# The row-column step of the expert stage: half of its products replaced by TensorE transposes

## The chip, the cores and the metric

The kernel runs on one core of a Trainium2 chip. The metric is the time of one launch on the device in microseconds. Engines are named as in the profile: PE (TensorE matmul), PEld (TensorE weight load), DVE (VectorE), ACT (ScalarE), POOL (GpSimd), SP (SyncE, here only the issuer of DMAs).

## What is computed

The input `x` holds 32 images of 64 channels and 56 by 56 positions, in float32. First comes a convolution block per image: a layer norm over the channels, a 3x3 convolution and a 1x1 convolution of signs with binarized weights, batch norms and leaky activations. Its result is added to `x`. Then each of the 100,352 positions is a token of 64 numbers that goes through a routed feed-forward layer with eight experts:

```python
logits = x @ gate_w + gate_b
probs = softmax(logits, axis=-1)
idx = argmax(probs, axis=-1)
...
hmid = relu(einsum('ecd,edf->ecf', buf, w1) + b1)   # 64 -> 256
ybuf = einsum('ecf,efd->ecd', hmid, w2) + b2         # 256 -> 64
y_tok = ybuf[idx, pos_g] * (prb * kept)
```

The result, scaled by the gate and with its infinities and NaNs replaced, is added to the tokens and stored in the layout of the images.

## The kernel before, in words

Two images form a pair: one lies on partitions 0 to 63, the other on 64 to 127. The first half of the program (up to some 970 us) does the convolution block for 16 pairs in a software pipeline, transposes the result to rows of tokens, routes them, and scatters *row pairs* to DRAM: a row pair is a token of the first image and the token of the second image at the same position. Row pairs are sorted by the two experts that they need, into groups (36 of them), each padded to blocks of 256 row pairs (SUPER = 256, in SUB = 2 parts of P = 128).

The second half is the **expert stage**: 231 blocks ("supers", NSUP), one after the other. Every engine runs its own `super_pass`, a software pipeline over the supers; the order of the work on an engine is written out by hand, and semaphores tie the engines together. In the pass k, PE (lines 810 to 845) does four steps:

- t, line 817, for super k+1: the **row-column step**. The rows of the super lie in SBUF as `RTH` (128 row pairs on the partitions; for each of the two images h, C = 64 numbers and three more). Four products with the identity matrix turn them into columns: for each part d and each image h, the 128x64 rows are the weights, the 128x128 identity is streamed, and the 64x128 result goes to the PSUM bank `PT`, image 0 on partitions 0 to 63 and image 1 on 64 to 127. The last product increments `s_pt`.
- l1, line 826, for super k: four products of the first expert layer, two for each image, with 64 rows of weights each (`HC` = 4). It waits until ACT has copied the columns of super k to `XT` (`s_xt`), and until ACT and DVE have emptied the hidden banks of super k-1 (`s_ha`, `s_hb`).
- l2, line 836, for super k-1: four products of the second layer, to 64 PSUM partitions each.
- back, line 844, for super k-2: two 128x128 transposes of the results, to rows.

A float32 product is carried out as two records of LDWEIGHTS and MATMUL, a float32 transpose as one: line 817 has 1848 records of each (231 x 4 x 2), line 844 has 462 (231 x 2).

Around them: SP loads the rows and the weights of a super twelve supers ahead (lines 600 to 610). ACT copies PT to XT (line 973), does three of the four ReLUs (line 980), adds the output bias (line 990) and widens the results (line 985). DVE does the fourth ReLU (line 1294) and the gating (lines 1307 to 1316). POOL scatters the results (line 524), held back by `s_pt` to a place six supers behind PE's row-column step. From super 62 on, seven of every twelve supers are followed on PE by an image group (`image_group`, line 855: four transposes of finished tokens back to image layout), whose sums DVE does (line 1323).

Of the kernel before, what the change touches and what calls it, by code (L numbers as in the profile page):

```python
# [14 lines left out]
def metaformer_kernel(nc, x, move1, w3, g1, be1, mu1, va1, pm1, ps1, pb1, move2, w_pw,  # L15
# [6 lines left out]
    IMAGES, C, H, W = x.shape  # L22
# [3 lines left out]
    P = 2 * C  # L26
# [83 lines left out]
    with ctx:  # L110
        def sb(name, shape, dt=fp32):
            return ctx.enter_context(nc.sbuf_tensor(name, shape, dt))
# [60 lines left out]
        ident = sb("ident", [P, P])  # L173
# [32 lines left out]
        RTH = RT.rearrange("p r j (h w) -> p r j h w", h=2)  # L206
# [119 lines left out]
        def wait(eng, s, count):  # L326

            if isinstance(count, int) and count <= 0:
                return
            eng.wait_ge(s, count)  # L330

        def wait_apart(eng, s, count):


            wait(eng, s, count)
            if not isinstance(count, int):
                eng.sem_inc(s_past, 1)
# [45 lines left out]
        def hidden(q):  # L383

            return (bank[2][:, 0:SUPER], bank[3][:, 0:SUPER], bank[2][:, SUPER:2 * SUPER], bank[4][:, 0:SUPER])[q]
# [283 lines left out]
        def _(pe):  # L669
            mm = nc.tensor.matmul  # L670
# [137 lines left out]
            PT, YT, YB = bank[0], bank[5], bank[7]  # L808

            def super_pass(k, ring, lap, t=True, l1=True, l2=True, back=True):  # L810
                if t:
                    u = (ring + 1) % RING
                    wait(pe, s_rt[u], (lap + (ring + 1) // RING) * 32 + 32)
                    wait_apart(pe, s_xt, k + 1)
                    for d in range(SUB):
                        for h in range(2):
                            last = mm(PT[h * C:h * C + C, d * P:(d + 1) * P], RTH[:, u, d, h, 0:C], ident[:, :],  # L817
                                      start=True, stop=True)
                    last.then_inc(s_pt, 1)
                if l1:  # L820
                    wait(pe, s_xt, k + 1)
                    wait(pe, s_ha, k)
                    wait(pe, s_hb, k)
                    for q in range(HC):
                        b = slice(q % 2 * C, q % 2 * C + C)
                        mm(hidden(q), WR[b, ring, q // 2 * P:(q // 2 + 1) * P], XT[b, ring % 2, :],  # L826
                           start=True, stop=True).then_inc(s_h, 1)
                if l2:
                    b = (ring - 1) % RING
                    wait(pe, s_ha, k)  # L830
                    wait(pe, s_hb, k)
                    wait(pe, s_ys, k - 1)
                    for q in range(HC):
                        h = q % 2
                        at = W2_AT + (h * KT + q // 2) * C
                        last = mm(YT[h * C:h * C + C, 0:SUPER], WR[:, b, at:at + C], HB[:, b % 2, q, :],  # L836
                                  start=q < 2, stop=q >= HC - 2)
                    last.then_inc(s_y, 1)
                if back:
                    b = ring % 2  # L840
                    wait(pe, s_ys, k - 1)
                    wait_apart(pe, s_g, (k - 3) * GSTEPS + 1)
                    for d in range(SUB):
                        last = nc.tensor.transpose(YB[:, d * P:(d + 1) * P], YS[:, b, d * P:(d + 1) * P], ident[:, :])  # L844
                    last.then_inc(s_yb, 1)
            super_pass(-1, -1 % RING, -1, l1=False, l2=False, back=False)
            super_pass(0, 0, 0, l2=False, back=False)
            super_pass(1, 1, 0, back=False)
            def image_group(q, odd, g):
                if g == 0:  # L850
# [517 lines left out]
```

## Time and profile before

| | |
|---|---|
| median of 3 runs (lowest to highest) | 1802.32 us (1801.11 to 1811.1) |
| profiled execution | 1805.56 us |
| its span, first to last instruction | 1803.6 us |
| PE busy | 1558.0 us (86%) |
| DVE busy | 1467.3 us (81%) |
| ACT busy | 1236.8 us (69%) |
| POOL busy | 1052.6 us (58%) |
| granted TensorE clock, mean | 0.921 |

The busy time of an engine is the part of the span in which one of its instructions is under way. Matmul records overlap, since the next one is streamed while the last one drains, and their ends are modelled; so on PE starts say more than ends. A timeline merges neighbouring records of one line and shape into one row with their count, the start of the first, and the time that they cover together. The granted clock is 1.00 at 2.4 GHz and 0.50 at 1.2 GHz.

### The profile page before, as it was taken

The numbers are of one execution on the slowest core, as the hardware profiler recorded it, in microseconds if no ns is written. First come the engines' busy times: TensorE is split into PE (matmuls) and PEld (weight loads), VectorE is DVE, ScalarE is ACT, GpSimd is POOL, SyncE is SP. The second block draws the span as 40 slices with busy tenths as digits, with TensorE's granted clock in tenths as the row PEclk, the third lists the DMA queues.
The fourth block names the chain that finished last, engine by engine and source line by source line (L and its number), as shares of the span: only waits on it lengthen the run. The fifth ranks groups of instructions, "written<-read, shape, count | busy, mean of one in ns | idle before, by whom it ended". The sixth has DMA issues, their size and how long they took to land.

```text
span 1803.6 us, 39937 instructions
## 1 busy us (share of the span) xinstructions
PE 1558.0 (86%) x10341; PEld 838.7 (47%) x10341; DVE 1467.3 (81%) x3641; ACT 1236.8 (69%) x4066; POOL 1052.6 (58%) x1052
## 2 busy tenths in 40 slices
PE   6998989888888898887740599999999999999994
PEld 1344434334343344443330355556666666666662
DVE  3588888888888888978882388889999999999995
ACT  4788786777777878777640377777676666776661
POOL 3115666666577666676667266666556565666662
PEclk8999988989998999987765799999999999999996
DMA  9446868676476773554422777788999999999995
GB/s 239 84 106 131 179 153 173 150 165 158 116 163 153 131 152 122 119 121 108 118 77 79 233 199 195 199 235 243 299 281 299 296 321 296 302 309 288 298 303 206
DMA packets 302219, 351.75 MB, mean 195 GB/s; under 512 B 48453, under 2 KB 252453, under 8 KB 295941
## 3 DMA queue, kind: packets, MB, share of 16 engines
q1 hardware_dynamic: 260644, 264.23, 55.6%
q0 software_dynamic: 41120, 85.81, 15.8%
q14 instruction: 101, 0.82, 0.1%
q8 instruction: 34, 0.56, 0.1%
q10 hardware_dynamic: 320, 0.33, 0.1%
HBM read 179.70 MB, written 180.01 MB: 199 GB/s over the span
## 4 chain that ended last, share of the span: by engine, by line
PE 49%; DVE 19%; issue 13%; POOL 8%; ACT 5%; DMA 4%; SPq 1%; POOLq 0%; ACTq 0%; DVEq 0%
PE bank L826 11%; PE bank L836 10%; PE bank L817 6%; POOL pairs_by_group L492 5%; PE bank L735 5%; PE bank L844 4%; PE bank L697 3%; PE bank L794 3%; DVE ROWS L1323 3%; DMA pairs_by_group<-ROWS,idx 2%; POOL X L486 2%; PE bank L745 2%; PE bank L768 2%; ACT SQR L960 1%; DVE X L1294 1%
## 5 line engine op out<-in xcount | busy, mean ns | idle before, releaser
L492 POOL DMA_INDIRECT pairs_by_group<-ROWS,idx x400 | 436.3, 1091 | 119.5 <-issue 113.2
L524 POOL DMA_INDIRECT results_by_pair<-X,PAIRNO x310 | 307.8, 993 | 220.6 <-PE bank L817 128.6
L980 ACT ACTIVATE X<-bank,X 128x256 f32<-128x256 f32 x693 | 283.7, 472 | 59.9 <-PE bank L826 59.9
L486 POOL TENSOR_TENSOR X<-Z,X 128x448 f32 (+1 forms) x112 | 140.2, 1252 | 268.6 <-DVE Z L1271 251.8
L826 PE MATMUL bank<-X 64*128 64x256 f32 x1848 | 263.4, 403 | 9.6 <-DVE X L1294 5.6
L836 PE MATMUL bank<-X 128*64 128x256 f32 x1848 | 250.4, 392 | 1.0 <-DVE X L1294 1.0
L735 PE MATMUL bank<-S,WB 128*128 128x448 bf16 x1008 | 231.6, 378 | 0.0
L973 ACT ACTIVATE X<-bank 128x256 f32<-128x256 f32 x231 | 88.8, 384 | 197.6 <-PE bank L817 196.7
L524 POOL DMA_INDIRECT results_by_pair<-S,PAIRNO x152 | 153.3, 1008 | 97.0 <-PE bank L817 70.2
L817 PE MATMUL bank<-ident,X 128*64 128x128 f32 x1848 | 153.3, 287 | 58.6 <-DMA X<-weights_by_group 58.1
L826 PEld LDWEIGHTS bank<-X 64*128 64x128 f32 x1848 | 163.1, 187 | 59.8 <-issue 46.3
L960 ACT ACTIVATE SQR<-bank 128x64 f32<-128x64 f32 (+1 forms) x800 | 168.8, 259 | 0.0
L960 ACT ACTIVATION_READ_ACCUMULATOR SQR<-bank 128x1 f32 (+1 forms) x800 | 167.1, 245 | 0.0
L735 PEld LDWEIGHTS bank<-S,WB 128*128 128x128 bf16 x1008 | 95.6, 102 | 152.6 <-issue 72.6
L836 PEld LDWEIGHTS bank<-X 128*64 128x64 f32 x1848 | 112.1, 136 | 110.8 <-issue 77.5
L1294 DVE TENSOR_SCALAR X<-bank,X 128x256 f32<-128x256 f32 x231 | 110.4, 478 | 60.7 <-PE bank L826 60.2
L697 PE MATMUL bank<-X,row_weights 128*128 (+1 forms) x224 | 126.7, 653 | 32.4 <-ACT SQ L908 23.6
L817 PEld LDWEIGHTS bank<-ident,X 128*64 128x64 f32 x1848 | 97.2, 137 | 95.3 <-DMA X<-weights_by_group 59.1
L764 PE MATMUL bank<-biasrow,ones 65*128 65x432 bf16 x144 | 51.6, 358 | 98.7 <-POOL X L486 50.3
L768 PE MATMUL bank<-row_weights,X 128*128 128x144 f32 x800 | 134.7, 308 | 0.0
L917 ACT ACTIVATE N<-Z,cst 128x448 f32 (+1 forms) x112 | 76.7, 685 | 84.1 <-DVE Z L1231 83.6
L768 PEld LDWEIGHTS bank<-row_weights,X 128*128 128x128 f32 x800 | 128.9, 209 | 5.1 <-issue 0.2
(213 smaller groups left out, 3045.9 us busy)
## 6 DMA issues: line engine op xcount, KB each, us to landing
X<-weights_by_group SPq DMA_DIRECT2D x231, 258.5 KB
X<-pairs_by_group SPq DMA_DIRECT2D x231, 134.0 KB
pairs_by_group<-PAD SPq DMA_DIRECT2D x15, 1742.0 KB
X<-in_x_dram SPq DMA_DIRECT2D x16, 1568.0 KB, 8.0
block_output<-X SPq DMA_DIRECT2D x112, 224.0 KB, 4.5
ROWS<-block_output SPq DMA_DIRECT2D x16, 1568.0 KB
Z<-results_by_pair SPq DMA_DIRECT2D x16, 1568.0 KB, 9.9
out_dram<-ROWS SPq DMA_DIRECT2D x16, 1568.0 KB
```

The source lines that it names most:

```text
L486: pool.tensor_tensor(X2[:, j * CW:(j + 1) * CW], Z[:, p.z(j * CW)], X[:, p.x(j * CW, CW)], ALU.add).then_inc(s_x2, 1)
L492: pool.indirect_dma_start(rows, bass.IndirectOffsetOnAxis(ap=idx[0:m, p.odd, k:k + 1], axis=0), ROWS[0:m, p.odd, k, :], None).then_inc(s_s ...
L524: pool.indirect_dma_start(done, bass.IndirectOffsetOnAxis(ap=PAIRNO[:, u, j:j + 1], axis=0), RES[u][:, j, :], None,).then_inc(s_back[u], 16)
L697: mm(centered(c, alone)[:, 0:CW], center[:, :], X[:, cen.x(c * CW, CW)], start=True, stop=True).then_inc(s_cen, 1)
L735: last = mm(CONV[(con.odd + c) % 2][:, 0:CW], WB[:, t, :], S1[:, con.odd, c * CHUNK_ROWS + dy:(c + 1) * CHUNK_ROWS + dy, dx:dx + W], start ...
L768: last = mm(ROWP[g][:, at:at + GW], X2[:, k * P:(k + 1) * P], row_weights[:, :], start=False, stop=k == group_tiles[g][-1])
L817: last = mm(PT[h * C:h * C + C, d * P:(d + 1) * P], RTH[:, u, d, h, 0:C], ident[:, :], start=True, stop=True)
L826: mm(hidden(q), WR[b, ring, q // 2 * P:(q // 2 + 1) * P], XT[b, ring % 2, :], start=True, stop=True).then_inc(s_h, 1)
L836: last = mm(YT[h * C:h * C + C, 0:SUPER], WR[:, b, at:at + C], HB[:, b % 2, q, :], start=q < 2, stop=q >= HC - 2)
L960: last = A(SQR[0:m, (odd * NG + g) % 2, i, h * C:h * C + C], src[0:m, i, h * C:h * C + C], ACT.Square, accum_out=SSQ[0:m, odd, k:k + 1])
L980: last = A(HB[:, ring % 2, q, :], hidden(q), ACT.Relu, bias=WR[:, ring, at:at + 1])
L1294: V.tensor_scalar(HB[:, ring % 2, q, :], hidden(q), WR[:, ring, at:at + 1], 0.0, ALU.add, ALU.max).then_inc(s_hb, 1)
```

## The change

In the row-column step, the two products of image 0 (h = 0) become two calls of TensorE's transpose, with the same operands and the same place in PSUM; the two products of image 1 stay. The order stays too: d = 0 with both images, then d = 1 with both images; the increment of `s_pt` stays on the last product.

```diff
                     wait_apart(pe, s_xt, k + 1)
                     for d in range(SUB):
                         for h in range(2):
-                            last = mm(PT[h * C:h * C + C, d * P:(d + 1) * P], RTH[:, u, d, h, 0:C], ident[:, :],
-                                      start=True, stop=True)
+                            if h == 0:
+                                nc.tensor.transpose(PT[0:C, d * P:(d + 1) * P], RTH[:, u, d, 0, 0:C], ident[:, :])
+                            else:
+                                last = mm(PT[C:P, d * P:(d + 1) * P], RTH[:, u, d, 1, 0:C], ident[:, :],
+                                          start=True, stop=True)
                     last.then_inc(s_pt, 1)
```

## Rows read from the trace of the kernel before

**Rows 1.** The page: span, busy time of PE, 40 slices of PE and its clock.
```profile
span 1803.6 us, 39937 instructions
...
PE 1558.0 (86%) x10341; PEld 838.7 (47%) x10341; DVE 1467.3 (81%) x3641; ACT 1236.8 (69%) x4066; POOL 1052.6 (58%) x1052
...
PE   6998989888888898887740599999999999999994
...
PEclk8999988989998999987765799999999999999996
```
**Rows 2.** Windows: from:to, length, busy of each engine (records), clock, DMA share, GB/s.
```profile
0.00:870.00 870.00, 755.62 (x3600) 342.41 (x3600) 703.42 (x1500) 654.56 (x2467) 502.43 (x506) 0.92 0.64 143
...
1011.00:1204.00 193.00, 192.16 (x1632) 113.90 (x1632) 153.71 (x483) 145.84 (x373) 113.83 (x117) 0.98 0.76 217
1204.00:1757.00 553.00, 544.03 (x4705) 340.28 (x4704) 506.47 (x1424) 384.16 (x998) 334.24 (x334) 1.00 0.93 294
```
**Rows 3.** Waits of PE, 1011 to 1757 us: total, times, longest.
```profile
PE bank L817 <- DMA X<-weights_by_group: 58.1, 1, 58.1
PE bank L826 <- DVE X L1294: 5.0, 12, 0.7
PE bank L826 <- ACT X L973: 2.8, 5, 0.6
```
**Rows 4.** Timeline of PE, a super without an image group: start, time covered, line.
```profile
1407.08 0.44 PE L844 MATMUL bank<-ident,X 128*128 128x128 f32 x2
1407.45 0.66 PE L817 MATMUL bank<-ident,X 128*64 128x128 f32 x8
1408.04 1.14 PE L826 MATMUL bank<-X 64*128 64x256 f32 x8
1409.10 1.08 PE L836 MATMUL bank<-X 128*64 128x256 f32 x8
1410.12 0.44 PE L844 MATMUL bank<-ident,X 128*128 128x128 f32 x2
```
**Rows 5.** Timeline of PE, a super with an image group.
```profile
1399.99 0.44 PE L844 MATMUL bank<-ident,X 128*128 128x128 f32 x2
1400.27 0.55 PE L855 MATMUL bank<-ident,Z 112*128 112x112 f32 x4
1400.75 0.66 PE L817 MATMUL bank<-ident,X 128*64 128x128 f32 x8
```
**Rows 6.** Timeline of PE at 703 us: float32 products on the whole array.
```profile
702.99 0.90 PE L768 MATMUL bank<-row_weights,X 128*128 128x144 f32 x6
```
**Rows 7.** Groups of instructions of PE, 702.75 to 704.9 us: busy, mean ns.
```profile
L768 PE MATMUL bank<-row_weights,X 128*128 128x144 f32 x12 | 1.8, 285 | 0.0
```
**Rows 8.** Groups of instructions of PE, 1204 to 1757 us.
```profile
L817 PE MATMUL bank<-ident,X 128*64 128x128 f32 x1328 | 109.2, 285 | 0.0
L844 PE MATMUL bank<-ident,X 128*128 128x128 f32 x334 | 73.0, 300 | 0.0
L855 PE MATMUL bank<-ident,Z 112*128 112x112 f32 x385 | 52.9, 259 | 0.0
```
**Rows 9.** Timeline of PE in the setup: products, then transposes, all 128 wide.
```profile
21.47 0.28 PE L681 MATMUL bank<-gw,row_weights 128*128 128x8 f32 x2
21.61 1.29 PE L686 MATMUL bank<-ident,X 128*128 128x128 f32 x10
```
**Rows 10.** Timeline of DVE: the same instruction in two supers with image groups.
```profile
1397.27 0.50 DVE L1294 TENSOR_SCALAR X<-bank,X 128x256 f32<-128x256 f32 x1
...
1400.81 0.50 DVE L1294 TENSOR_SCALAR X<-bank,X 128x256 f32<-128x256 f32 x1
```
**Rows 11.** Waits of ACT, 1011 to 1757 us.
```profile
ACT X L973 <- PE bank L817: 195.9, 225, 62.1
```
**Rows 12.** Waits of DVE, 1011 to 1757 us.
```profile
DVE N L1307 <- PE bank L844: 39.3, 125, 0.9
```

## The prediction

> **What bounds the kernel now.** I first read the page, the busy times and the slices [rows 1]: PE is at nine tenths in every slice from about 1010 us to the end of the expert stage, and its clock in these slices stands at nine or more. The windows by stage sharpen that [rows 2]: between 1204 and 1757 us PE is busy for 544 of 553 us at a granted clock of 1.00 (the 2.4 GHz level); DVE comes next with 506. Then the waits of PE [rows 3]: apart from one wait of 58.1 us for the first weights, PE waits 7.8 us in the whole stage. So each nanosecond that PE gains or loses per super counts once per super, 231 times, until DVE or a DMA takes over.
>
> Last the timelines, which give one super as steps between starts [rows 4]: L844 0.37 us (1407.08 to 1407.45), L817 0.59, L826 1.06, L836 1.02. Together that is 3.04, and an image group adds 0.38: from the L844 of rows 5 to the L817 behind it is 0.76, against 0.37. The change edits L817, 0.59 of 3.04 us.
>
> **How the 0.59 us is made.** Three readings price it.
>
> - A pass (one MATMUL record) over the whole array: six float32 passes of L768 with 144 columns cover 0.90 us, one alone 0.285 [rows 6, 7], so the starts are (0.90 - 0.285) / 5 = 0.123 us apart, 0.109 for 128 columns. The transposes agree: four of L855 with 112 columns add 0.38 us [rows 5], 0.095 each, 0.109 for 128.
> - L817 does not keep that pace: its eight passes cover 0.66 us, one 0.285 [rows 4, 8], so starts are 0.054 us apart on average, half of 0.109. Nothing but the array's halves explains that: the products of image 0 end on PSUM partitions 0 to 63, those of image 1 on 64 to 127, and **the two run side by side**. Eight passes are four slots of 0.109.
> - What is left of a step is a fixed charge: L817 0.59 - 4 x 0.109 = 0.15, L844 0.37 - 2 x 0.109 = 0.15, L836 (256 columns, four slots of 0.218) 1.02 - 0.87 = 0.15, L826 1.06 - 0.87 = 0.19. Between L844 and L855 there is none (the four transposes cost 0.095 each and nothing else). The rows that pay differ in the shape that the array is used in (128*128, 128*64, 64*128); the two that don't pay both use all columns. So the charge of 0.15 us comes **with a change of shape**, not with a new line; and not with a change from product to transpose either, since in the setup L686 starts 0.14 us after L681 although two products of eight columns and a weight load lie between [rows 9].
>
> **The change, part by part.** Removed per super: two products of image 0, four passes with their weight loads. Added: two transposes of one pass each (L844 has one record per transpose [rows 8]: 334 for 167 supers). Nothing is moved, no DMA, no wait and no semaphore count changes.
>
> *The removed passes* are worth nothing by themselves: each stood beside a pass of image 1, whose chain of four slots (0.436 us) stays. That is the cover; if it were gone, they would cost 0.053 us apiece.
>
> *The added transposes* hang on one unknown: whether a transpose with 64 columns of weights can use one half of the array, beside products in the other. No row shows one; every transpose in these rows loads 128 columns and takes the whole array. The ends: zero, if it runs beside the products (the slots stay four), or the whole array each time, with a change of shape before and behind. I take the second, since the nearest rows, L844 and L855, are float32 transposes in this same stage with the same identity and the whole array.
>
> The Trainium skill, page "TensorEngine Tiling (Array Packing)", section "Restrictions", states that column tiling disables the transpose mode for float32 input. No row here shows it. By that page the first rival below can't happen; neither the sum nor the chances use it.
>
> Then PE's order per super is: L844's two transposes and, in the same shape, the first new one: +0.109, no charge. The product of d = 0, alone in its half: 0.15 + 2 x 0.109 = 0.37. The second transpose: 0.15 + 0.109 = 0.26. The product of d = 1: 0.37. Together 1.11 in place of 0.59: **+0.51 us per super** with unrounded terms (1.104 - 0.59). 231 x 0.514 = 118.7 us.
>
> *What it gives back.* PE's waits for DVE and ACT vanish in a longer super. In the window of rows 2, 166 supers (1328 / 8) and 96 image groups (385 / 4) [rows 8] make 166 x 3.04 + 96 x 0.38 = 541 us of 553: 12 us of waits, the listed 7.8 among them. They come with the image groups, where DVE needs 3.54 us from L1294 to L1294 [rows 10] against 3.42 for PE; afterwards PE needs 3.93 there, so DVE keeps up. I take back 12 us. Sum: 118.7 - 12 = **+107 us**.
>
> *Who waits for the longer step.* `s_pt` comes 0.51 us later: ACT's L973 waits for it, and L980, L990 and L985 are queued behind it on ACT. Today L973 idles 195.9 us for L817 [rows 11], and its XT is read only one super later; it moves with PE. DVE's L1307 waits 39.3 us for L844 [rows 12] and will wait longer. POOL's scatters follow `s_pt`. SP's loads run twelve supers ahead, and DMA share falls from 0.93 as the supers get longer. Nothing is late next: PE is the bound by more than before.
>
> The profiled execution took 1805.56 us, 3.2 over the median of 1802.32. 1805.6 + 107 = 1912.6 for such an execution; against the median 1909, and I write **1908 us** (the steps are read to 0.01 us).
>
> **The rivals.** A measurement of this kernel tells about 0.5% (9 us) from no change.
>
> 1. *Side by side* (not slower). A 64-column transpose uses its half while image 1's passes run in the other. Place: L817. Price: zero, the four slots of image 1 stay 0.436 us and the step 0.59. It decides as soon as a transpose starts while a product of image 1 is under way. For it: the halves run like that today, and going from product to transpose costs nothing in rows 9. Against: no transpose of the trace does it. Time 1802, 1800 to 1806. The same holds if the calls were carried out as products after all; one record per transpose in L844 speaks against that. 8%.
> 2. *Same shape, but each alone.* No change of shape, but a transpose and a product never overlap: 0.109 + 0.218, twice, is 0.654 in place of 0.436: +0.218 x 231 - 12 = +38, 1840. Nothing in the trace shows such a pair. 5%.
> 3. *A pass is 0.054 us of its own* (faster). If eight passes of L817 ran one after the other, six would take 2 x 0.053 less: -0.106 x 231 = -24, 1778. Against it: a pass of the same width takes twice that wherever the whole array is used [rows 5 to 7]. 2%. The Trainium skill, page "Perfetto Trace Analysis", section "Transposes", says that a logical transpose should use the transpose and not a matmul, because it skips the arithmetic. By that page the change would be a gain; the rows give a transpose one pass for a product's two, but with the two images side by side that saves no slot.
> 4. *The clock falls.* The shape changes add idle moments: six charges of 0.15 per super in place of four. If the stage got the 0.92 of the first 870 us instead of 1.00 [rows 2], its 746 us plus 107 would take 1 / 0.92 times as long, +74: 1982. Against it: with four charges of 0.15 in 3.04 us the clock is 1.00 throughout. 3%.
>
> **How the numbers follow.** The forecast has 82%: the rows price every piece, and only the use of the whole array is inferred. Its own ends: if one of the three new charges were free (a turn back from transpose to product that the trace doesn't show by itself), 0.15 x 231 = 35 less, 1873; if no wait is given back, 1920, and with one charge at L826's 0.19, 9 more, about 1930. The range 1875 to 1930 therefore holds what the forecast covers and leaves out the four rivals. Slower by over 0.5%: 82 + 5 + 3 = 90%. Same: 8%. Faster: 2%.
>
> **What would show it.** Right: two groups where L817 was, 462 transposes and 924 product passes; the timeline shows them in turns and not side by side, the two steps together about 1.1 us from the end of L844 or L855 to L826; period 3.55 without and 3.93 with an image group; L826's waits for DVE and ACT near zero; the first half of the program unchanged; DMA share of the stage near 0.82. Wrong: transposes that start within the products of image 1 with the period still 3.04 (rival 1); a step near 0.8 (rival 2); a clock under 1.00 in the stage (rival 4); or DVE or DMA waits that grow on PE.

## The result, and the profile after

The changed kernel takes **1898.6 us** (median of 4 runs, 1895.12 to 1903.02) against 1801.88 us (4 runs of the kernel before): 96.7 us more, a ratio of 1.0547 with a 95% interval of 1.0503 to 1.0592. The forecast was 1908 us, in a range of 1875 to 1930. The profiled execution took 1903.02 us, its span is 1901.1 us.

The page of the changed kernel: busy times, and the two groups that stand where L817 stood (all later lines moved down by three: L826 is now L829, L836 L839, L844 L847, L855 L858).

```profile
span 1901.1 us, 39013 instructions
...
PE 1673.7 (88%) x9879; PEld 875.3 (46%) x9879; DVE 1474.0 (78%) x3641; ACT 1229.3 (65%) x4066; POOL 1040.2 (55%) x1052
...
L820 PE MATMUL bank<-ident,X 128*64 128x128 f32 x924 | 201.6, 300 | 0.0
...
L818 PE MATMUL bank<-ident,X 128*64 128x128 f32 x462 | 133.4, 289 | 57.3 <-DMA X<-weights_by_group 56.8
```

PE has 462 records fewer than before (9879 against 10341) and is busy for 116 us more. The windows of the same stretches as in [rows 2] show where:

```profile
0.00:870.00 870.00, 760.67 (x3608) 346.04 (x3609) 705.38 (x1510) 657.08 (x2481) 501.48 (x507) 0.92 0.58 143
...
1204.00:1757.00 553.00, 553.00 (x3892) 321.32 (x3889) 454.56 (x1268) 340.04 (x894) 289.85 (x298) 1.00 0.84 258
```

The first half is as it was: the same clock of 0.92 and the same 143 GB/s (the share of the DMA engines reads 0.58 where it was 0.64). In the expert stage PE is now busy without a gap, at the same granted clock of 1.00, and DVE, ACT, POOL and the DMA engines all do less in the same 553 us. The timeline of PE in a super without an image group, which answers to [rows 4]:

```profile
1107.34 0.44 PE L847 MATMUL bank<-ident,X 128*128 128x128 f32 x2
1107.61 0.27 PE L818 MATMUL bank<-ident,X 128*64 128x128 f32 x1
1107.82 0.43 PE L820 MATMUL bank<-ident,X 128*64 128x128 f32 x2
1108.18 0.30 PE L818 MATMUL bank<-ident,X 128*64 128x128 f32 x1
1108.41 0.43 PE L820 MATMUL bank<-ident,X 128*64 128x128 f32 x2
1108.77 1.14 PE L829 MATMUL bank<-X 64*128 64x256 f32 x8
1109.84 1.08 PE L839 MATMUL bank<-X 128*64 128x256 f32 x8
1110.85 0.44 PE L847 MATMUL bank<-ident,X 128*128 128x128 f32 x2
```

Transposes (L818) and products (L820) take turns; below, a turn is a change from one to the other. From L847 to L829 it is now 1.43 us (1107.34 to 1108.77), where L844 to L826 was 0.96: **0.47 us more**. The steps: L847's two transposes with the first new one 0.48, the first product 0.36, the second transpose 0.23, the second product 0.36. The whole super takes 3.51 us instead of 3.04. With an image group it is 3.90, from one L847 to the next:

```profile
1450.33 0.44 PE L847 MATMUL bank<-ident,X 128*128 128x128 f32 x2
1454.23 0.44 PE L847 MATMUL bank<-ident,X 128*128 128x128 f32 x2
```

The waits of PE in the whole stage, which answer to [rows 3]; behind the first supers nothing is left of the 7.8 us for DVE and ACT at l1 (L829):

```profile
PE bank L818 <- DMA X<-weights_by_group: 56.8, 1, 56.8
PE bank L818 <- ACT X L976: 0.6, 1, 0.6
```

So 0.47 x 231 = 109 us more on PE, less the 12 us of waits that [rows 2] and [rows 8] gave, make 97 us; measured were 96.7.

### The profile page after: what moved, and what is told of

Read it like the earlier page. It is cut to its first block, busy times and chain, and to the rows that moved or that the text cites. A ratio compares the mean times of both kernels' runs of the same rounds, so it can differ in the third digit from the quotient of the medians.

```text
span 1901.1 us, 39013 instructions
## 1 busy us (share of the span) xinstructions
PE 1673.7 (88%) x9879; PEld 875.3 (46%) x9879; DVE 1474.0 (78%) x3641; ACT 1229.3 (65%) x4066; POOL 1040.2 (55%) x1052
## 4 chain that ended last, share of the span: by engine, by line
PE 62%; DVE 11%; issue 11%; POOL 8%; ACT 5%; DMA 2%; SPq 1%; POOLq 0%; ACTq 0%; DVEq 0%
PE bank L829 13%; PE bank L839 12%; PE bank L820 9%; POOL pairs_by_group L492 5%; PE bank L847 4%; PE bank L818 4%; PE bank L735 4%; PE bank L697 3%; PE bank L794 3%; POOL X L486 2%; PE bank L745 2%; PE bank L858 2%; PE bank L768 2%; ACT SQR L963 1%; DVE Z L1258 1%
## 5 line engine op out<-in xcount | busy, mean ns | idle before, releaser
L524 POOL DMA_INDIRECT results_by_pair<-X,PAIRNO x310 | 303.1, 978 | 296.3 <-PE bank L820 240.6
L829 PE MATMUL bank<-X 64*128 64x256 f32 x1848 | 263.9, 404 | 0.0
L839 PE MATMUL bank<-X 128*64 128x256 f32 x1848 | 251.3, 393 | 1.2 <-DVE X L1297 1.2
L524 POOL DMA_INDIRECT results_by_pair<-S,PAIRNO x152 | 148.3, 976 | 132.4 <-PE bank L820 107.9
L820 PE MATMUL bank<-ident,X 128*64 128x128 f32 x924 | 201.6, 300 | 0.0
L1310 DVE TENSOR_TENSOR N<-bank,X 128x256 f32<-128x256 f32 x231 | 98.1, 425 | 128.6 <-PE bank L847 127.8
L818 PE MATMUL bank<-ident,X 128*64 128x128 f32 x462 | 133.4, 289 | 57.3 <-DMA X<-weights_by_group 56.8
L829 PEld LDWEIGHTS bank<-X 64*128 64x128 f32 x1848 | 160.0, 187 | 50.4 <-issue 39.7
L839 PEld LDWEIGHTS bank<-X 128*64 128x64 f32 x1848 | 112.5, 136 | 111.4 <-issue 78.3
L768 PE MATMUL bank<-row_weights,X 128*128 128x144 f32 x800 | 139.5, 316 | 0.0
L768 PEld LDWEIGHTS bank<-row_weights,X 128*128 128x128 f32 x800 | 133.4, 215 | 4.9
```

Of the source, the lines that this page charges most:

```text
L524: pool.indirect_dma_start(done, bass.IndirectOffsetOnAxis(ap=PAIRNO[:, u, j:j + 1], axis=0), RES[u][:, j, :], None,).then_inc(s_back[u], 16)
L768: last = mm(ROWP[g][:, at:at + GW], X2[:, k * P:(k + 1) * P], row_weights[:, :], start=False, stop=k == group_tiles[g][-1])
L818: nc.tensor.transpose(PT[0:C, d * P:(d + 1) * P], RTH[:, u, d, 0, 0:C], ident[:, :])
L820: last = mm(PT[C:P, d * P:(d + 1) * P], RTH[:, u, d, 1, 0:C], ident[:, :], start=True, stop=True)
```

## The experiments

The kernels of the experiments differ from the kernel before in the row-column step alone, unless said. The cuts of code are shortened: the first four are against the changed kernel (e1_grouped's in words), those of e6_shifted and e7_less_dve against e5_two_covers. The start of the expert stage moves from run to run, whatever the kernel (more on this at the end), so the stage is read by itself too: from the first to the last MATMUL record of the transposes in the back step (L844 in the kernel before). In the kernel before and in the changed one it is 746.2 and 842.6 us; the columns of these rows are the count, the shortest, median and longest duration in ns, and the first and last start in us.

```profile
L844 PE MATMUL bank<-ident,X x462: 272/300/332, 1022.0 to 1768.2; 128*128 128x128 f32 x154
```

```profile
L847 PE MATMUL bank<-ident,X x462: 272/300/330, 1023.0 to 1865.6; 128*128 128x128 f32 x154
```

### e1_grouped: the same four operations, ordered by kind

```diff
-for d in range(SUB):
-    transpose(image 0, part d)
-    last = mm(image 1, part d)
+for d in range(SUB):
+    transpose(image 0, part d)
+for d in range(SUB):
+    last = mm(image 1, part d)
```

> Both transposes of image 0 first, then both products of image 1; nothing else differs from the changed kernel. Theory (a float32 transpose takes the whole array, and the charge of some 0.15 us belongs to each change of the array's shape): both transposes go into the shape of L844 at 0.11 us each, the products are one step of 0.59 us as before; a super of 3.03 + 0.22 = 3.25 us without an image group, time about 1840 us. Rival (the charge belongs to each 64-column transpose wherever it stands): no different from the changed kernel, 3.51 us a super, 1899 us. Rival (charge per product that runs without a partner): also no different from the changed kernel.

The timeline of PE in e1_grouped, a super without an image group:

```profile
1107.45 0.44 PE L845 MATMUL bank<-ident,X 128*128 128x128 f32 x2
1107.73 0.38 PE L816 MATMUL bank<-ident,X 128*64 128x128 f32 x2
1108.04 0.65 PE L818 MATMUL bank<-ident,X 128*64 128x128 f32 x4
1108.62 1.14 PE L827 MATMUL bank<-X 64*128 64x256 f32 x8
1109.68 1.08 PE L837 MATMUL bank<-X 128*64 128x256 f32 x8
1110.70 0.44 PE L845 MATMUL bank<-ident,X 128*128 128x128 f32 x2
```

Four transposes in a row take 0.59 us from L845 to L818, 0.22 more than L844's two alone; the two products of image 1 without partners take 0.58, as the step took before with partners. The super is 3.25 us. Median 1841.45 us, measured beside the kernel before on a chip on which that took 1809.38: 32 us more, ratio 1.0136 (1.0061 to 1.0212). The expected 1840 us was 38 more than 1801.88, so it is partly luck that the two times agree. The stage goes from 1039.3 to 1821.3 us, 35.8 longer than before; 231 x 0.21 less the 12 us of waits is 36. The same two transposes and two products, put in another order, are 0.26 us a super cheaper than in the changed kernel. So the charge is neither the transpose's own, nor that of a product without a partner: it comes with the turns. That the products alone take 0.58 shows too that the four passes taken away had been worth nothing.

### e3_wide_product: no transpose, but the whole array

```diff
-transpose(PT[0:C, d * P:(d + 1) * P], RTH[:, u, d, 0, 0:C], ident[:, :])
+mm(PT[0:C + 1, d * P:(d + 1) * P], RTH[:, u, d, 0, 0:C + 1], ident[:, :],
+   start=True, stop=True)
```

> In the changed kernel each transpose is replaced by a product of 65 columns of weights (image 0 and one number more, whose row image 1's product then overwrites), which uses the whole array like a transpose but takes two passes. Theory (change of shape): the same turns as in the changed kernel, plus one pass of 0.11 us for each of the two: 3.51 + 0.22 = 3.73 us a super without an image group, up to 3.8 with longer weight loads, time about 1950 us. Rival (the turn between transpose and product drains the array, whatever the shape): no such turns, eight passes in a row behind one charge, about 1.0 us from L844 to L826 and 3.47 us a super, time about 1890 us.

The timeline of PE in e3_wide_product:

```profile
1109.48 0.44 PE L845 MATMUL bank<-ident,X 128*128 128x128 f32 x2
1109.75 0.38 PE L816 MATMUL bank<-ident,X 128*65 128x128 f32 x2
1110.07 0.43 PE L818 MATMUL bank<-ident,X 128*64 128x128 f32 x2
1110.43 0.43 PE L816 MATMUL bank<-ident,X 128*65 128x128 f32 x2
1110.79 0.43 PE L818 MATMUL bank<-ident,X 128*64 128x128 f32 x2
1111.15 0.70 PE L827 MATMUL bank<-X 64*128 64x256 f32 x4
...
1113.23 0.44 PE L845 MATMUL bank<-ident,X 128*128 128x128 f32 x2
```

Products of 65 columns beside products of 64 take the same turns: from L845 to L827 1.67 us, 0.24 more than in the changed kernel, of which 0.22 is the second pass of each wide product. The super is 3.75 us, one run took 1957.65 us. A turn costs at least as much between two kinds of product, so no transpose is needed for the charge.

### e4_half_transpose: a transpose that fits in half of the array

```diff
-transpose(PT[0:C, d * P:(d + 1) * P], RTH[:, u, d, 0, 0:C], ident[:, :])
+if isinstance(k, int) and k == -1:
+    mm(PT[0:C, d * P:(d + 1) * P], RTH[:, u, d, 0, 0:C], ident[:, :], start=True, stop=True)
+else:
+    transpose(PT[0:C, SUPER + d * C:SUPER + (d + 1) * C].bitcast(bf16), bf16_constant[:, d, :], identb[:, :])
```

The bfloat16 identity `identb` is filled once in the setup, which is not shown here.

> In the changed kernel the two float32 transposes are replaced by bfloat16 transposes of a constant with 64 columns, into a spare place of PSUM; image 0's columns are formed once, for the first super, and kept for all others, so image 0's rows are left out of the computation. A bfloat16 transpose may use half of the array. Theory (change of shape): no turn, the transposes lie beside image 1's products: step 0.59 us, super 3.03 us, time about 1802 us. Rival (transpose against product drains whatever the shape): turns as in the changed kernel, 3.4 us a super or more, time 1880 us or more. Between them (no turn, but never side by side): 2 x 0.05 us more, 3.14 us a super, about 1820 us.

The timeline of PE in e4_half_transpose:

```profile
1108.97 0.44 PE L852 MATMUL bank<-ident,X 128*128 128x128 f32 x2
1109.34 0.24 PE L823 MATMUL bank<-identb,upper 128*64 128x128 bf16 x1
1109.34 0.32 PE L825 MATMUL bank<-ident,X 128*64 128x128 f32 x1
1109.42 0.22 PE L823 MATMUL bank<-identb,upper 128*64 128x128 bf16 x1
1109.50 0.49 PE L825 MATMUL bank<-ident,X 128*64 128x128 f32 x3
1109.92 1.14 PE L834 MATMUL bank<-X 64*128 64x256 f32 x8
```

The bfloat16 transposes (L823) start at 1109.34 and 1109.42, the first float32 pass of image 1 (L825) at 1109.34: side by side. From L852 to L834 it is 0.95 us, as before the change (0.96), and the stage lasts 747.4 us (1042.3 to 1789.7) against 746.2. The run as a whole took 1827.63 us, because its expert stage started 20 us later than that of the kernel before. So a bfloat16 transpose and a float32 product don't disturb each other as such. With e3_wide_product this is a pair of opposites: products that take the whole array pay, transposes that stay in their half don't. This kernel alone also changed the number format of the transpose; but the row-column step of e3_wide_product is all float32 and has no transpose, and in [rows 9] the float32 transposes start 0.14 us after the first of two float32 products in the whole array, which leaves no room for a charge of 0.15. The shape is what is paid for.

### e5_two_covers and e5_again: transposes alone

If a transpose in the shape of L844 costs one pass and no charge, the step can do without products. 128 columns of weights that end with image 1's 64 put these on rows 64 to 127 of PT; a second transpose of 64 columns, with its result from row 0 on as in the changed kernel, then puts image 0 over rows 0 to 63.

```diff
-transpose(PT[0:C, d * P:(d + 1) * P], RTH[:, u, d, 0, 0:C], ident[:, :])
-last = mm(PT[C:P, d * P:(d + 1) * P], RTH[:, u, d, 1, 0:C], ident[:, :],
-          start=True, stop=True)
+transpose(PT[:, d * P:(d + 1) * P], RT[:, u, d, UNIT - C:UNIT + C], ident[:, :])
+last = transpose(PT[0:C, d * P:(d + 1) * P], RTH[:, u, d, 0, 0:C], ident[:, :])
```

> No product left in the row-column step: for each part a transpose of 128 columns that end with image 1's 64 (its rows 64 to 127 are image 1's columns), and then the 64-column transpose of image 0, which overwrites rows 0 to 63. Theory (change of shape): all four passes stand in the shape of L844, 4 x 0.11 us and no charge of their own, 0.15 us less than the 0.59 us before: 2.88 us a super without an image group; with image groups DVE, which needs 3.53 us there, sets the pace; time 1765 to 1785 us, faster than both kernels. Rival (the charge belongs to each 64-column transpose): 2 x 0.2 us more, 3.25 us a super, time 1840 us or more.

> The kernel with four transposes and no product in the row-column step once more, in more rounds. Theory (its gain is 9 us in the supers without image groups and some 4 us in those with them, where DVE sets the pace): some 13 to 17 us less than the kernel before, ratio 0.990 to 0.993. Rival (the first reading was the spread of the first half of the program): ratio 1.00.

The timeline of PE in e5_again:

```profile
1107.64 0.44 PE L843 MATMUL bank<-ident,X 128*128 128x128 f32 x2
1107.91 0.27 PE L816 MATMUL bank<-ident,X 128*128 128x128 f32 x1
1108.02 0.27 PE L817 MATMUL bank<-ident,X 128*64 128x128 f32 x1
1108.13 0.27 PE L816 MATMUL bank<-ident,X 128*128 128x128 f32 x1
1108.24 0.27 PE L817 MATMUL bank<-ident,X 128*64 128x128 f32 x1
1108.44 1.14 PE L825 MATMUL bank<-X 64*128 64x256 f32 x8
```

The starts are 0.11 us apart, 64 columns of weights beside 128 without a charge. So the float32 transposes of 64 columns run in the shape of the 128-column ones, although the profile prints 128*64 for them as for the products. And from L843 to L825 it is 0.80 us, 0.16 less than before the change. Medians are 1792.94 us beside 1809.38 for the kernel before, ratio 0.9885 (0.9813 to 0.9957), and 1785.57 us beside 1799.43 in e5_again, ratio 0.992 (0.9876 to 0.9964): **faster than both kernels**, by less than the first expectation of 1765 to 1785 us and in line with the second. The stage is 732.9 us, 13.3 less than before: the 61 supers ahead of the image groups give 0.15 each, some 9 us, and all others together only some 4. The gain is nearly gone where the image groups begin. Starts of L843 twelve supers apart in e5_again (39.76 us), and of L844 in the kernel before (40.09 us):

```profile
1389.88 0.44 PE L843 MATMUL bank<-ident,X 128*128 128x128 f32 x2
...
1429.64 0.44 PE L843 MATMUL bank<-ident,X 128*128 128x128 f32 x2
```

```profile
1407.08 0.44 PE L844 MATMUL bank<-ident,X 128*128 128x128 f32 x2
...
1447.17 0.44 PE L844 MATMUL bank<-ident,X 128*128 128x128 f32 x2
```

The waits of PE in e5_two_covers say for whom:

```profile
PE bank L825 <- DVE X L1293: 25.7, 69, 0.7
```

### e6_shifted: half as many transposes

```diff
-transpose(PT[:, d * P:(d + 1) * P], RT[:, u, d, UNIT - C:UNIT + C], ident[:, :])
-last = transpose(PT[0:C, d * P:(d + 1) * P], RTH[:, u, d, 0, 0:C], ident[:, :])
+last = transpose(PT[:, d * P:(d + 1) * P], RT[:, u, d, 0:P], ident[:, :])
```

> The whole row-column step as two 128-column transposes of neighbouring numbers; image 1's columns come out shifted by three, so the experts work on other numbers there. Theory (PE sets the pace without image groups, DVE with them): two passes of 0.11 us less than with four transposes, 2.88 - 0.22 = 2.66 us a super without an image group; twelve supers with seven image groups stay at 39.7 us; time 13 us under that of the four transposes. Rival (PE sets the pace throughout): 2.6 us less for twelve supers as well, some 50 us under it.

One run took 1784.42 us, with the expert stage starting 14.5 us later than in e5_again (1029.9 against 1015.4); the stage lasted 717.1 us, 15.8 less than the 732.9 of e5_again. The size is near what the theory gave, but by luck: the places are others. Waits of PE in e6_shifted, and its window without image groups:

```profile
PE bank L824 <- DVE X L1292: 37.1, 84, 0.8
PE bank L824 <- ACT X L971: 10.0, 19, 0.6
```

```profile
1040.00:1190.00 150.00, 144.95 (x1072) 88.44 (x1068) 136.00 (x428) 116.49 (x321) 109.41 (x108) 1.00 0.80 220
```

A super has 20 records of PE here, so 1072 records in 150 us are 53.6 supers of 2.80 us, not 2.66: below some 2.8 us PE waits for DVE and ACT even without image groups. With them twelve supers take 38.92 us (from the L842 at 1409.51 to that at 1448.43), 0.8 less than in e5_again where I had expected none. So of the 15.8 us some 5 (61 x 0.08) came ahead of the image groups, where I had expected 13, and some 11 behind that (some 14 times twelve supers, 0.8 each). PE, 0.22 us shorter per super, is not what sets the pace in either part.

### e7_less_dve: the suspect of the image groups

```diff
-gstep(V.scalar_tensor_tensor(out=SGN[:], in0=Y2[:], scalar=0.0, in1=SGN[:], op0=ALU.is_lt, op1=ALU.subtract))
...
-GSTEPS = 4
+GSTEPS = 3
```

> The four transposes, and on DVE the step that gives negative infinities their sign left out (0.43 us of DVE per super; finite results are the same). Theory (DVE sets the pace in the supers with image groups): these come down to PE's 2.88 + 0.38 = 3.27 us, twelve supers to about 37.3 us from 39.7, time about 30 us under that of the four transposes. Rival (a DMA sets the pace there): twelve supers stay near 39.7 us and the time the same.

Starts of L843 in e7_less_dve, twelve supers apart:

```profile
1408.78 0.44 PE L843 MATMUL bank<-ident,X 128*128 128x128 f32 x2
...
1446.10 0.44 PE L843 MATMUL bank<-ident,X 128*128 128x128 f32 x2
```

Twelve supers take 37.32 us, as expected of PE alone, and the stage 698.7 us (1011.9 to 1710.6), 34.2 less than with the instruction. Median 1753.72 us, 32 less than e5_again measured beside it, ratio to the kernel before 0.9758 (0.97 to 0.9816). The DMA engines were not the bound: their share from 1204 to 1700 us is 0.93 in e5_again and rises to 0.98 here. What this kernel leaves out matters only to results that are not finite; I show it as a measurement of DVE, not as a version.

## Why the prediction was right

- **PE bounds the stage, so a longer step counts once per super.** Right: the stage grew by 96.4 us, the span by 97.5, and PE's waits for DVE and ACT behind the first supers are gone.
- **The two images ran side by side, so the passes removed are worth nothing.** Right, by e1_grouped: image 1's products alone take 0.58 us, with partners they took 0.59.
- **The transposes take the whole array.** This was the step that rested on the nearest rows alone. In the changed kernel no L818 starts beside an L820, while the bfloat16 transposes of e4_half_transpose do start beside the products. The Trainium skill, page "TensorEngine Tiling (Array Packing)", section "Restrictions", lists the transpose mode for float32 input among what column tiling disables; the two traces agree (1.43 us with float32 against 0.95 with bfloat16, from the back step to l1). That the transpose then takes the whole array is shown by e1_grouped and e5_again: beside 128-column transposes it pays no charge.
- **The charge comes with the change of shape.** Right, by the pair e3_wide_product (products that use the whole array: same turns, 3.75 us a super) and e4_half_transpose (transposes in their half: none, 0.95 us). The rival of a turn between transpose and product would have put e3_wide_product at 3.47 us.
- **The sum.** The mechanism was right and the size a little high. The forecast of +107 us came out at +96.7. The term that was mis-sized is the second transpose, "0.15 + 0.109 = 0.26": it measured 0.23. The products, put at 0.37, measured 0.36. Together the step is 0.47 us longer and not 0.51; 0.04 x 231 is 9 of the 10 us. The 12 us of waits given back were right.
- **The rivals.** Side by side and "each alone" fall with the timeline of the changed kernel (1.43 us, where they would have left 0.96 and 1.18). The clock stayed at 1.00. Fewer passes did not make it faster: the Trainium skill, page "Perfetto Trace Analysis", section "Transposes", advises a transpose for what is logically one; here that cost 96.7 us, and e5_two_covers shows a case in which it pays: there it saves a change of shape instead of adding two.
- **What I watched for.** Periods of 3.51 and 3.90 us where 3.55 and 3.93 were named, the two steps together 1.06 us (1.43 less the 0.37 of the back step) where 1.1 was, and a DMA share of 0.84 where 0.82 was.

## What to carry to other kernels

On a TensorE that is the bound, count the changes of shape between neighbouring products (128*128, 128*64, 64*128) and not only the passes: here each cost 0.12 to 0.19 us, more than a pass of 128 columns (0.11). Take the shape from the starts and not from the printed one alone: the float32 transposes of 64 columns are printed as 128*64 and behave as 128*128. Before replacing one of two half-array products, look whether its partner runs beside it; then removing it gains nothing. If a step's neighbour already uses the whole array, staying in that shape can be cheaper than running halves side by side, even where it moves some numbers twice, as the four transposes of e5_two_covers did.

## What was not expected of the hardware

- A turn to a 64-column transpose costs less than one to a product: 0.23 us less one pass of 0.11 leaves 0.12, where products and 128-column transposes leave 0.14 to 0.15. The timeline of e5_again shows that a charge has two parts: 0.09 us before the new shape starts (the last L817 to L825 is 0.20, a pass is 0.11) and, in the shape of L843, 0.05 behind its first pass (L843 to L816 is 0.27, two passes are 0.22). Of the 0.12 that leaves 0.03 for the second part, and the weight loads of e4_half_transpose point to why: the second load of 64 columns for a transpose starts 0.03 us after the first (1109.34 to 1109.37), the one for a float32 product 0.05 us (1109.34 to 1109.39). Those transposes are in bfloat16 and the turn in question is to float32 ones, so the reason is not shown.

```profile
1109.34 0.11 PEld L823 LDWEIGHTS bank<-identb,upper 128*64 128x64 bf16 x1 [0.17 <-issue]
1109.34 0.13 PEld L825 LDWEIGHTS bank<-ident,X 128*64 128x64 f32 x1
1109.37 0.11 PEld L823 LDWEIGHTS bank<-identb,upper 128*64 128x64 bf16 x1
1109.39 0.35 PEld L825 LDWEIGHTS bank<-ident,X 128*64 128x64 f32 x3
```

- A transpose in bfloat16 and a product in float32 ran at the same time in the two halves of the array, into one PSUM bank.
- The start of the expert stage moved between 1011.9 and 1042.3 us (first back step) in the profiles of kernels whose first half does the same work, while the stage was 732.9 us in both profiles of the four transposes. (e4_half_transpose also fills `identb` in its setup.) The granted clock goes with it: from 40 to 60 us it is 0.50 (the 1.2 GHz level) in the four profiles whose stage starts latest (e5_two_covers, e6_shifted, e1_grouped, e4_half_transpose: 1026.9 to 1042.3) and 0.65 to 1.00 in the other five (1011.9 to 1023.1). Why it is low there in those four stays open.
